# Half of each adapter unit's loads issued by ScalarE: a two-layer kernel on one core

## What is computed

```python
sign = 2 * mask - 1                                          # mask: (8, 1024, 1024) int32
x = x + (x @ W.T + bias) + coeff[b] * (x[b] @ sign[b])       # layer 1
x = x + x @ weight[ids[b]].T                                 # layer 2; weight: (8, 1024, 1024)
```

## Time and profile before

| | |
|---|---|
| median of 3 runs | 422.8 us (422.68 to 423.53) |
| the profiled execution's own time | 423.07 us |
| its span, first to last instruction | 421.3 us |
| PE busy | 390.4 us (93%) |
| DVE busy | 366.6 us (87%) |
| ACT busy | 258.0 us (61%) |
| mean granted PE clock | 0.992 |
| DMA | 88.54 MB, 210 GB/s on average |

### The profile page before, as it was taken

The page is one execution under the profiler, slowest core; times in us unless marked ns, Lnnn a source line. Parts: engine busy times, 40 slices in busy tenths (PEclk is TensorE's granted clock), DMA queues, the critical chain, the costliest instruction groups (busy, mean ns, idle before and its releaser), DMA issues.

```text
span 421.3 us, 6999 instructions
## 1 busy us (share of the span) xinstructions
PE 390.4 (93%) x2496; PEld 354.8 (84%) x2496; DVE 366.6 (87%) x400; ACT 258.0 (61%) x313; POOL 6.0 (1%) x14
## 2 busy tenths in 40 slices
PE   1979749999999999999999999999999999999777
PEld 1878748999899998999999998999999998999655
DVE  0455899999999999999999999999999999998740
ACT  3476765666676766667566766667566676665321
POOL 1111000000000000000000000000000000000000
PEclk9999979999999999999999999999999999999999
DMA  7998996988579874999779995999479975545211
GB/s 225 273 323 285 226 222 167 276 230 222 167 206 286 252 215 126 269 233 237 188 213 244 231 245 167 281 244 239 148 234 271 248 186 172 155 142 174 83 50 50
DMA packets 62451, 88.54 MB, mean 210 GB/s; under 512 B 7122, under 2 KB 48082, under 8 KB 62418
## 3 DMA queue, kind: packets, MB, share of 16 engines
q1 hardware_dynamic: 62418, 88.11, 78.9%
HBM read 79.70 MB, written 8.39 MB: 209 GB/s over the span
## 4 chain that ended last, share of the span: by engine, by line
PE 66%; DVE 18%; ACT 8%; DMA 3%; issue 2%; SPq 1%; ACTq 0%; DVEq 0%
PE first_ps L243 34%; PE second_ps L260 30%; DVE h_lo L396 6%; DVE natural L380 4%; DVE masks L360 4%; ACT masks L290 3%; DVE M_lo L365 2%; PE turn_ps L227 2%; DMA x_nat<-in_x_dram 2%; DVE w_lo L384 2%; ACT h_hi L316 1%; ACT w_hi L305 1%; DMA natural<-in_L_cond_weight_dram 1%; ACT M_hi L297 1%; ACT out_sb L323 1%
## 5 line engine op out<-in xcount | busy, mean ns | idle before, releaser
L243 PE MATMUL first_ps<-x_lo,M_hi 128*128 128x256 f32 x512 | 147.6, 288 | 10.0 <-DVE h_lo L396 6.0
L243 PE MATMUL first_ps<-x_hi,M_hi 128*128 128x256 f32 x512 | 145.6, 284 | 0.0
L243 PE MATMUL first_ps<-x_hi,M_lo 128*128 128x256 f32 x512 | 145.5, 284 | 0.0
L297 ACT CAST M_hi<-masks 128x1024 fp32r<-128x1024 f32 x64 | 67.2, 1050 | 117.6 <-DVE masks L360 117.6
L243 PEld LDWEIGHTS first_ps<-x_lo,M_hi 128*128 128x128 f32 x512 | 98.9, 193 | 13.2 <-issue 6.2
L260 PE MATMUL second_ps<-w_hi,h_lo 128*128 128x512 f32 x256 | 100.2, 391 | 5.0 <-DVE w_lo L384 2.8
L260 PE MATMUL second_ps<-w_hi,h_hi 128*128 128x512 f32 x256 | 99.9, 390 | 0.0
L243 PEld LDWEIGHTS first_ps<-x_hi,M_hi 128*128 128x128 f32 x512 | 98.9, 193 | 1.1
L260 PE MATMUL second_ps<-w_lo,h_hi 128*128 128x512 f32 x256 | 99.6, 389 | 0.0
L243 PEld LDWEIGHTS first_ps<-x_hi,M_lo 128*128 128x128 f32 x512 | 98.8, 193 | 0.0
L360 DVE SCALAR_TENSOR_TENSOR masks<-masks,coeffs,WT 128x1024 f32<-128x1024 f32 x64 | 81.8, 1278 | 13.0 <-ACT masks L290 9.5
(11 more groups left out here) (16 smaller groups left out, 128.1 us busy)
## 6 DMA issues: line engine op xcount, KB each, us to landing
masks<-in_mask_Bx4096x_ik_dram SPq DMA_DIRECT2D x64, 512.0 KB, 6.6
natural<-in_L_cond_weight_dram SPq DMA_DIRECT2D x256, 128.0 KB, 3.8
x_nat<-in_x_dram SPq DMA_DIRECT2D x8, 1024.0 KB, 7.8
out_dram<-out_sb SPq DMA_DIRECT2D x32, 256.0 KB, 3.3
natural<-in_L_cond_W_dram SPq DMA_DIRECT2D x8, 512.0 KB, 7.8
bias_col<-in_L_cond_b_dram SPq DMA_DIRECT2D x4, 1.0 KB, 5.3
coeffs<-in_condB_coeff_dram SPq DMA_DIRECT2D x1, 4.0 KB, 4.7
ids_row<-in_itok_B_dram SPq DMA_DIRECT2D x1, 0.0 KB
```

What stands on the lines that cost most here:

```text
L243: done = nc.tensor.matmul(acc(u), left, right, start=(k == 0 and u % 2 == 0 and j == 0), stop=(k == K - 1 and u % 2 == 1 and j == 2))
L297: nc.scalar.copy(by_chunk(M_hi, n), by_quadrant(masks[:, n % RING, :].bitcast(F32))).then_inc(M_hi_done, 1)
```

## The change

SP issues only the first two quadrants of each unit. ACT gets a function of its own that reads the adapter number into one of its registers and issues the other two from ACT's queue. It stands at the head of ACT's iteration, ahead of `round_M(n+1)`, behind the same waits as on SP. The semaphore of the slot still counts four DMAs.

```diff
@@ SyncE, load_unit(g)
-                for a in range(GRP):
+                for a in range(GRP // 2):
                     sp.dma_start(natural[a * SQ:(a + 1) * SQ, g % RING, :].rearrange("r (c f) -> r c f", f=Q),
@@ ScalarE
+            def load_unit_rest(g):
+                who = act.value_load(ids_row[0:1, g // K:g // K + 1], min_val=0, max_val=weight.shape[0] - 1)
+                m = g % K
+                for a in range(GRP // 2, GRP):
+                    nc.scalar.dma_start(natural[a * SQ:(a + 1) * SQ, g % RING, :].rearrange("r (c f) -> r c f", f=Q),
+                                        weight[bass.ds(who, 1), m * P:(m + 1) * P, a * Q:(a + 1) * Q]
+                                        .rearrange("a (c r) f -> r (a c) f", r=SQ)).then_inc(natural_loaded[g % RING], DMA)
@@ ScalarE, in the loop over n
                 b, i = n // K, n % K
+                if n == 4:
+                    act.wait_ge(ids_loaded, DMA)
+                if n in (4, 5):
+                    for g in (2 * n - 8, 2 * n - 7):
+                        act.wait_ge(W_turned, RING + g + 1)
+                        load_unit_rest(g)
+                elif n > 5 and n - 2 < CHUNKS:
+                    act.wait_ge(w_done, n - 5)
+                    load_unit_rest(n - 2)
                 if n + 1 < CHUNKS:
                     round_M(n + 1)
```

## The result

The changed kernel takes 440.8 us (median of 4 runs, 440.1 to 441.9) against 423.2 us of the kernel before (4 runs, 422.7 to 423.5). The ratio is 1.041, with a 95% interval of 1.038 to 1.045. The forecast was 442.3 us. The loss comes for the most part from the batches: five times in each, ACT issues its two DMAs ahead of the one result that DVE is waiting for, and DVE had no time to spare there.

What follows compares the result with a forecast made beforehand. The prediction took DVE, back to back without slack, to bound the kernel. Batches 1 to 6 (16.2), last batch (0.7), tail (0.5) and start (2.1) sum to 19.5 us, giving 442.3 us, 4.6% slower; range 429 to 452.

Steps and rivals of the forecast that it cites:

- What bounds the kernel: Batches: DVE stands back to back, 5.11 us an iteration, 47.0 us a batch; a DVE delay lengthens the batch in full.
- rival 4: Batches: PE sets the pace, so the delay is absorbed until its queue is empty; 430 us, chance 0.10.
- The price of an iteration: ACT ahead of round_M: 0.75 us wait and register, 0.83 DMAs, 0.10 handover, 0.09 interference; delay 0.54 us.
- The interference: SP and ACT issuing at the same moment: ACT's two DMAs wait 0 to 0.2 us, 0.09 taken.
- rival 2: SP and ACT issuing: they lock each other out in full, delay 0.90 us an iteration; 455.9 us, chance 0.15.
- How many iterations: Batches 1 to 6: 5 of 8 iterations exposed, none behind rest_x or rest_h; 6 x 5 x 0.54 = 16.2 us.
- The last batch: Batch 7: three exposed iterations less the spare time, 3 x 0.54 - 0.9 = 0.7 us lost.
- the pace changes hands: Batch 7: no later DVE work hangs on it; PE runs without a stop to the end of layer 1.
- the 0.9 us at `first(61)`: Batch 7: rest_M(61) ends at 370.33, first(61) starts at about 371.2, so 0.9 us are spare.
- The tail: After the batches: the last unit's issuing stands in front of round_w(60) in a serial chain; 0.5 us more.
- The start: At n = 4 and 5 ACT's issuing delays round_M(5) and round_M(6); 2.1 us lost, between 1.2 and 3.4.
- the wait for the data gone: Start: the unit's data land before the late rest_M(6), so DVE's 0.96 us DMA wait is given back.

Runs made afterwards that it cites:

- start_only: Against the kernel before: ACT issues two quadrants of units 0 to 3 only, SP all four from unit 4 on; 425.6 us, ratio 1.005.
- start_last_two: Against the kernel before: ACT issues two quadrants of units 2 and 3 only (n = 5), SP all others; 425.1 us, ratio 1.003.
- start_first_two: Against the kernel before: ACT issues two quadrants of units 0 and 1 only (n = 4), SP all others; 426.9 us, ratio 1.007.
- steady_late: Against the changed kernel: SP alone issues units 0 to 3; ACT's later wait and issue stand at the end of its iteration; 423.3 us.
- sp_later: Against the changed kernel: SP alone issues units 0 to 3; later SP's half waits until ACT's round_M(n+1) is done; 440.1 us.
- reg_first: Against the changed kernel: SP alone issues units 0 to 3; later ACT loads its register before the wait for the slot; 423.9 us.

## Why the prediction was right, and where it wasn't

**What bounds the kernel.** Right. A delay of DVE lengthened each batch, with PE waiting for `M_lo` behind it, and rival 4 (absorption) is refuted: six batches together took 14.0 us more, twice the 7 us of its whole sum, and `start_only` kept its 2 us to the end.

**The price of an iteration.** Predicted 0.75 + 0.83 + 0.10 + 0.09 = 1.77 us, measured 0.70 + 0.92 + 0.10 = 1.72 us. DVE's plain iteration grew by 0.51 us (5.62 - 5.11), where 0.54 was predicted; in the profile it is a wait of 0.34 to 0.48 us in 31 of 35 iterations. SP's rows were a good price for ACT. The interference is real (375 against 328 ns on ACT; SP's own median went from 317 to 324) and small; the full lock of rival 2 would have shown 640 ns. For the Trainium skill's rule of a descriptor generator locked for exclusive use (Perfetto Trace Analysis, DMA Instruction — HWDGE (DVE, Sync)) the trace agrees that two issuers hinder each other, but not for a whole instruction: 0.05 us of 0.32 us is what the other issuer can be seen to cost in the median.

**How many iterations.** Right: 30 in batches 1 to 6, 5 in the last, none behind `rest_x` or `rest_h`. Their sum is 14.0 us for 16.2: thirty waits of 15.4 us together, 1.2 us for thirty times the 0.04 us named above, less 2.6 us at `rest_x`. Two terms of it, of opposite sign, the prediction lacked: slow DMAs and the time at `rest_x`. The four iterations that aren't plain waited 0.65, 0.72, 1.17 and 1.47 us. At the third of them both sequencers stood at their DMAs:

```profile
235.58 1.64 ACTq L288 DMA_DIRECT2D natural<-in_L_cond_weight_dram  x2
```

```profile
235.61 1.62 SPq L145 DMA_DIRECT2D natural<-in_L_cond_weight_dram  x2
```

SP's rows of before had such outliers (1836 ns at most); on SP they were free, on ACT they are not. In the other direction, the 0.2 us for which DVE waited at each `rest_x` are gone: DVE arrives later and finds `x_hi` ready. That absorbs 0.4 us of each batch.

**The last batch.** The step that failed is that "the pace changes hands", from DVE to PE: 0.7 us predicted, 1.6 measured. For PE alone the 0.7 is about right. Its last chunk of layer 1 ends where `second` takes over, at 385.14 before and 401.79 in the changed kernel:

```profile
385.14 0.40 PE L260 MATMUL second_ps<-w_hi,h_lo 128*128 128x512 f32 x1
```

```profile
401.79 0.40 PE L260 MATMUL second_ps<-w_hi,h_lo 128*128 128x512 f32 x1
```

Counted from the `rest_h` that opens the batch (341.69 and 357.71), that is 43.45 and 44.08 us, 0.6 more. But PE no longer decides when `rest_h` can start. DVE, in the changed kernel, goes from `rest_w` into `rest_h` without a gap:

```profile
402.57 1.23 DVE L401 TENSOR_TENSOR w_lo<-natural,w_hi 128x1024 fp32r<-128x1024 f32 x1 [1.28 <-ACT w_hi L313]
403.80 3.23 DVE L413 SCALAR_TENSOR_TENSOR h_lo<-first_ps,bias_col,h_hi 128x256 fp32r<-128x256 f32 x8
```

Before, DVE waited 1.1 us for `h_hi` here, and that was the slack, not the 0.9 us at `first(61)`. Five waits (2.2 us) and 0.5 us at this `rest_w` less 1.1 make the 1.6. ACT's side is as late:

```profile
400.52 0.92 ACTq L288 DMA_DIRECT2D natural<-in_L_cond_weight_dram  x2
401.49 1.05 ACT L313 CAST w_hi<-natural 128x1024 fp32r<-128x1024 f32 x1 [3.55 <-DVE natural L397]
402.44 0.58 ACT L331 COPY out_sb<-second_ps 128x512 f32<-128x512 f32 x1
402.92 1.94 ACT L324 ACTIVATE h_hi<-first_ps,bias_col 128x256 fp32r<-128x256 f32 x5
```

The issuing stands in front of `round_w`, and `round_h` starts 1.1 us after PE is through. The prediction had this issuing in the tail only. I looked for the spare time at the chunk in the middle and not at the end of the stretch.

**The tail.** 0.5 us predicted, 0.5 measured; DVE's wait for `w_hi` is 1.34 us at that unit instead of 0.80.

**The start.** The sum, 2.1 us, agrees with 2.0 and is right for wrong reasons. Predicted was `round_M(5)` 0.9 to 1.9 us late, `round_M(6)` at 45.8, and the wait for the data gone. The changed kernel has:

```profile
34.90 0.89 ACTq L288 DMA_DIRECT2D natural<-in_L_cond_weight_dram  x2
...
38.08 1.05 ACT L305 CAST M_hi<-masks 128x1024 fp32r<-128x1024 f32 x1 [1.42 <-DVE masks L377]
...
44.44 1.05 ACT L305 CAST M_hi<-masks 128x1024 fp32r<-128x1024 f32 x1 [3.45 <-issue]
```

```profile
45.21 0.28 DVE L393 TENSOR_TENSOR natural<-natural,ident 32x128 f32<-32x128 f32 x1 [2.84 <-DMA natural<-in_L_cond_weight_dram]
```

ACT's sequencer ran ahead by a whole `copy_WT` and more, issuing from 34.9 us under the casts, so `round_M(5)` is not late. `round_M(6)` is, by 1.7 us. And the wait for data, which I had as the one gain of the change, grew from 0.2 and 0.96 us to 2.8 us. The two experiments on the start show that the data bind, in `start_last_two` by 0.65 us ahead of the late `round_M(6)`. Why ACT's loads, issued from 2.6 us ahead of SP's in `start_first_two`, hold up SP's by 3 to 6 us is open: the share of busy DMA engines is near 1 there in both kernels (0.96 before, 1.08 in `start_first_two`, 24 to 44 us), and I made no run that separates the order of the queues from the amount in flight.

The mean granted clock of PE was 0.977 in the changed kernel against 0.992; it doesn't explain the loss, since `steady_late` has 0.979 and loses nothing.

## What to carry to other kernels

An engine at 61% can have no slack at the place where a change puts work. Ask when its next result is due and what releases the work: here 1.23 us lay between the release and the due time, issuing and handover that fit into it were free, and each DMA beyond that cost its 0.42 to 0.47 us in full, in five iterations of eight. DMAs issued by a compute engine belong behind the instructions that someone waits for, and register loads ahead of the wait. In a crowded start, loads that one queue issues early can hold up those that are needed first on the other; issuing them in the order in which they are needed looks like the remedy, but no run here tried it.

## What the runs showed that I had not expected

- A register load from the on-chip memory isn't constant: 280 ns as a rule, but 450 to 759 ns in 17 of 60 iterations of `sp_later`, with nothing changed on ACT, and as slow in 14 of `steady_late` and 9 of `reg_first`. It costs time only where someone waits.
- Two DMA queues are not neutral in a crowded stretch: ACT's four loads from 35.1 us on (landing after 3.8 to 7.3 us) went with a landing of SP's after as much as 10.0 us, where it was about 3.2. Over a whole run nothing of the kind is seen: the median is 3.8 us before, and 3.1 (ACT) and 3.3 us (SP) in the changed kernel.
- A slot of 0.03 us between two engines, repeated at every step of a timeline, is a sign of two chains of equal length. Here it told more about the cost of the change than any busy share.
